# A decoder layer's context maxima reduced over the partitions by TensorE and two small transfers, and the second half's x transposed through another PSUM bank

## The chip, the core and the metric

The kernel runs on one core of a Trainium2 chip. The number that counts is the device time of one execution in microseconds (us). Five engines share the work: PE (TensorE, matrix products and transpositions), DVE (VectorE), ACT (ScalarE), POOL (GpSimd) and SP, which here only issues transfers. Each runs its own program in order; they meet at semaphores. PSUM has eight banks, `bank[0]` to `bank[7]`, into which PE writes and which DVE and ACT read.

## What is computed

One pre-norm decoder layer over x of 4 batches by 512 tokens by 512 channels, in float32:

```python
x = x + attention(layernorm(x), wq, wk, wv, wo)   # 32 query heads, 8 key heads, causal, rotary
x = x + cross(layernorm(x), ctx)                  # below
x = x + moe(layernorm(x), ...)                    # 8 experts and a shared one

def cross(x, w):                                  # w is ctx: 4 matrices of 512x512
    amax = max(abs(xb), axis=-1)                  # per row, blocks of 128
    xq = round_to_fp8(xb * 448 / amax) * amax / 448
    amax = max(abs(wb), axis=(2, 4))              # one maximum for each 128x128 block of ctx
    wq = round_to_fp8(wb * 448 / amax) * amax / 448
    return einsum("emk,enk->emn", xq, wq)
```

The change touches the maxima of the 128x128 blocks of ctx, and the layer norm's transposition of x for the attention of batches 2 and 3.

## The kernel before, in words

**Steps.** The attention is a loop over `h` from -8 to 134, written out in every engine's program; one pass is called a step here, and step `h` works on several heads at once. There are 128 pairs of a head and a batch (below: heads), in 32 units of four heads (`NU`). In step h, PE computes the scores of head h in four pieces (L435, L436), six of the products for the coming unit's queries, keys and values over a unit's four steps of three (L417 to L419 from `XT`, `Wh`, `Wl`), the weighted values of head h-3 (`weigh`, L474, L475, into bank 5), the transpositions of the probabilities of head h-2 (`turn_p`, L459, parts 0, 1 and 2 in banks 2, 3 and 4) and the output product of head h-7 (`attn_out`, L417 to L419 from `Oh`, into bank 5). DVE begins step h with the reciprocal of head h-1's sums (L1027), which makes the start of that row the mark of a step in what follows; then it masks the scores (L1038), joins the weighted values (`join`, L1073), splits the turned probabilities (L1079), rotates queries (L1051) and adds the output product to X (L1088). ACT takes exponentials (L762) and the high parts of splits. POOL scales the probabilities (`normalised`, L1444, four instructions for a head), and takes the low parts of several splits. Nothing plans this order: it is what the loops say, and the semaphores (`need.wait_ge`) hold it together. A counter such as `v_x` is raised by one for each output product added to X.

**The maxima of ctx.** 16 tiles of ctx are loaded into `xnx` one after another. `context_max` (L1112, DVE) takes the maximum of each row in four blocks, into `wam`, 128 partitions by 64. After the last, POOL in step 45 makes the maximum over all partitions of all 64 columns with one `partition_all_reduce` (L1577), so that every partition has all 64 maxima in `wsc`. In step 49 DVE makes scales and their inverses of them (`context_scales`, L1091 to L1096). They are first needed in step 62 (`scaled`, L784).

**x of batches 2 and 3.** `XT[0]` holds the transposed x of batches 0 and then 2, `XT[1]` of 1 and then 3. In steps 51 to 58 DVE normalises one tile of 128 tokens (`first_norm`, L987, into `xnx`), in steps 52 to 59 PE transposes it (`first_turn`, L414, recorded on L409, four transpositions), and ACT (L713) and DVE (L1009) split it into `XT`. The transposition goes into bank 5, just after `attn_out` wrote into the same bank: so it waits until DVE has added that product to X (`wait_bank5`, user "first_turn", L367). In the next step `weigh` writes bank 5 and waits for the split (L374). Unit 16, whose products begin in step 56, needs the four tiles of batch 2 (`wait_xt` in `project`, L485), and unit 17, in step 60, those of batch 3.

**SP.** In each unit it issues the transfers that put keys and queries in place: `turn_keys`, `place_queries` twice (eight issues each), `double_keys`, besides loads of weights.

Of the kernel before, what the change touches and what calls it, by code (L numbers as in the profile page):

```python
# [15 lines left out]
NCTX = 16  # L16
NSAVE = NG


# [59 lines left out]
def decoder(nc, x_in, ctx_in, wqkv_in, wo_in, wg_in, wf_in, ident_in, mask_in, rope_in, ksin_in, rank_in, tri_in, out):  # L79
# [3 lines left out]
    with ExitStack() as root:  # L83
        scope = [root]

        def sem(name):
            return root.enter_context(nc.semaphore(name))

        def sb(name, shape, dt=F32):
# [91 lines left out]
        kept = nc.dram_tensor("kept", (NCTX * 128, D), F32).ap()  # L181
        saved = nc.dram_tensor("saved", (NSAVE, 2, 128, 4, 384), F32).ap()
        oe = nc.dram_tensor("oe", (NE * CAP, D), F32).ap()
        G = [XN[:, k, :] for k in range(TB)] + CW + T1
# [28 lines left out]
            sem(f"v_{n}") for n in ("own", "xn", "xt", "wq", "wo", "ri", "mask", "ra", "rb", "k1", "vl", "join", "pt", "x"))  # L213
        v_bm, v_bq, g_badd, g_bq = sem("v_bm"), sem("v_bq"), sem("g_badd"), sem("g_bq")
        v_cmax, v_cscale, v_q, v_turn, v_x2, v_xn3, v_lt, v_cum, v_place, v_idx, v_piece, v_hm, v_h, v_x3, v_out = (
            sem(f"v_{n}") for n in ("cmax", "cscale", "q", "turn", "x2", "xn3", "lt", "cum", "place", "idx", "piece",
                                    "hm", "h", "x3", "out"))

        g_own, g_pad, g_wq, g_wo, g_norm, g_rot, g_ql, g_ks, g_k, g_kl, g_o, g_zero, g_call, g_t2, g_q, g_const, g_piece = (
            sem(f"g_{n}") for n in ("own", "pad", "wq", "wo", "norm", "rot", "ql", "ks", "k", "kl", "o", "zero", "call", "t2", "q",  # L220
                                    "const", "piece"))
# [139 lines left out]
        def wait_bank5(need, h, user):  # L361

            if user == "attn_out":
                need.wait_ge(a_tmp, h - 2)
                need.wait_ge(v_join, h - 2)
            elif user == "first_turn":
                need.wait_ge(v_x, h - 6)  # L367
            elif h == 3:
                wait_xt(need, 6)
            elif h < 8 or h - 8 >= NH - 11:  # L370
                need.wait_ge(a_tmp, h - 3)
                need.wait_ge(v_join, h - 3)
            elif 52 <= h - 1 < 60:
                wait_xt(need, h - 44)  # L374
            else:
                need.wait_ge(v_x, h - 7)
# [26 lines left out]
        def tensor_engine(e):  # L403
# [34 lines left out]
            def turn_v(u):  # L438
# [8 lines left out]
                last.then_inc(p_vt, 1)  # L447

            def turn_p(h, part):
                ps = bank[2 + part]  # L450
                need.wait_ge(g_norm, 4 * h + 4)
                if h:
                    need.wait_ge(a_pt, 3 * (h - 1) + part + 1)
                    need.wait_ge(v_pt, 3 * (h - 1) + part + 1)
                else:
                    wait_xt(need, 2 * TB)
                for m, (kb, qb) in enumerate(PT_BLOCKS[part]):
                    src = P[:, h % 3, off[qb] + kb * 128:off[qb] + (kb + 1) * 128]
                    last = e.transpose(ps[:, tokens(m)], src, ident[:, :])  # L459
                last.then_inc(p_pt, 1)  # L460
# [189 lines left out]
            for h in range(-8, NH + 7):  # L650
# [22 lines left out]
                if after_unit and k == 1:  # L673
                    need.wait_ge(v_vl, unit)
                if 0 <= h - 2 < NH:
                    turn_p(h - 2, 2)
# [9 lines left out]
                if 52 <= h < 60:  # L686
                    wait_bank5(need, h, "first_turn")
                    first_turn(h - 44, 5)
            for s in (-8, -7, -6):
# [15 lines left out]
        def scalar_engine(e):  # L705
# [172 lines left out]
            for h in range(-8, NH + 7):  # L878
# [48 lines left out]
                if 52 <= h < 60:  # L927
                    first_turn(h - 44, 5)
                if h > NH + 2:
# [26 lines left out]
        def vector_engine(e):  # L956
# [153 lines left out]
            def context_max(m):  # L1110
                need.wait_ge(d_by[m % 2], 16 * (m // 2 + 1))
                e.tensor_reduce(wam[:, m, :], four(xnx[:, m % 2, :]), AX.X, ALU.max,  # L1112
                                apply_absolute_value=True).then_inc(v_cmax, 1)

            def context_scales():
                need.wait_ge(g_call, 1)
                scales(wsc[:, 0, :], wsc[:, 1, :], wsc[:, 0, :], 1e-6).then_inc(v_cscale, 1)
# [217 lines left out]
            for h in range(-8, NH + 7):  # L1335
# [8 lines left out]
                if h in takes:  # L1344
                    context_max(takes[h])
                if h == 49:
                    context_scales()
# [27 lines left out]
                if 0 <= h - 2 < NH:  # L1375
                    pt_lo(h - 2, 1)
                    pt_lo(h - 2, 2)
                if unit < NU and k in (1, 2):
                    rotate(unit, k - 1, 0)
# [12 lines left out]
                if 52 <= h < 60:  # L1392
                    first_turn(h - 44, 5)
                if h > NH + 2:
# [25 lines left out]
        def gpsimd_engine(e):  # L1420
# [129 lines left out]
            for h in range(-8, NH + 7):  # L1550
# [22 lines left out]
                if unit < NU and k == 3:  # L1573
                    rotate(unit)
                if h == 45:
                    need.wait_ge(v_cmax, NCTX)
                    e.partition_all_reduce(wsc[:, 0, :], wam[:, :, :].rearrange("p i c -> p (i c)"), 128,  # L1577
                                           bass.bass_isa.ReduceOp.max).then_inc(g_call, 1)
                if h - 4 in begins:
# [31 lines left out]
        def sync_engine(e):  # L1611
# [138 lines left out]
            for h in range(-8, NH + 7):  # L1750
# [28 lines left out]
                if h in begins:  # L1779
                    load_background(NCTX + begins[h])  # L1780
                if 8 <= h < 24:
                    need.wait_ge(g_zero, 1)
                    e.dma_start(xdz[h - 8], Zb[:, 0, :]).then_inc(d_zero, 16)
# [106 lines left out]
```

## Time and profile before

| what | us |
|---|---|
| median of 3 runs | 1612.51 |
| lowest, highest | 1610.12, 1615.79 |
| the profiled execution | 1612.85 |
| its span in the trace | 1611.0 |
| of it the attention's steps, first to last reciprocal | from 62.5 to about 1040 |

The rest of the time, 1.85 us in the profiled execution, lies around the span. The attention's steps take about 60% of the span; behind them come the cross product and the experts, where the change alters nothing. In the trace a row of an engine tells when an instruction started, how long it took, and in brackets how long the engine had been idle before it and what it waited for.

### The profile page before, as it was taken

What the parts mean: (1) busy time and instruction counts of PE and PEld (TensorE: products, weight loads), DVE (VectorE), ACT (ScalarE), POOL (GpSimd) and SP (SyncE); (2) the same over time, 40 slices, a digit from 0 to 9 for tenths busy, and PEclk for the clock granted to TensorE, in tenths of its full rate; (3) what the DMA queues carried; (4) which work ended last, traced back from release to release, by engine and by line L of the source; (5) the groups of instructions that cost most, each with busy time, mean ns of one, the idle gap of its engine ahead of it and who ended that gap; (6) DMA issues with size and microseconds to landing.
All of it is one profiled execution on the core that took longest, in us unless ns stands there. A gap on an engine that the chain in (4) does not pass through costs nothing.

```text
span 1611.0 us, 26917 instructions
## 1 busy us (share of the span) xinstructions
PE 1465.1 (91%) x8616; PEld 1280.9 (80%) x8616; DVE 1213.7 (75%) x2951; ACT 948.4 (59%) x2384; POOL 1020.4 (63%) x1007
## 2 busy tenths in 40 slices
PE   5799999999798999999999998676989899899997
PEld 4588888887677888888888887565788888799996
DVE  6678888887777777878878787986767665587785
ACT  2477787776466678877878878523121213565662
POOL 1687887885776788888888888642303132354555
PEclk9899999999899999999999999897899999899998
DMA  5345444333132334334434433123010002577777
GB/s 188 98 126 165 135 134 134 109 87 100 49 102 50 88 85 118 98 90 115 113 81 109 120 81 89 33 88 91 27 27 27 8 27 84 176 240 221 227 217 239
DMA packets 106588, 177.04 MB, mean 110 GB/s; under 512 B 16662, under 2 KB 38422, under 8 KB 106448
## 3 DMA queue, kind: packets, MB, share of 16 engines
q1 hardware_dynamic: 103888, 167.07, 35.8%
q0 software_dynamic: 2560, 8.25, 1.6%
q8 instruction: 70, 1.15, 0.3%
q14 instruction: 70, 0.57, 0.1%
HBM read 97.28 MB, written 31.98 MB: 80 GB/s over the span
## 4 chain that ended last, share of the span: by engine, by line
PE 68%; DVE 14%; ACT 7%; issue 5%; DMA 2%; POOL 2%; SPq 1%; DVEq 0%; ACTq 0%; POOLq 0%
PE bank L417 15%; PE bank L419 14%; PE bank L418 14%; PE bank L459 6%; PE bank L435 4%; PE bank L474 4%; PE bank L475 4%; PE bank L436 4%; ACT P L762 3%; PE bank L409 2%; DVE P L1038 2%; DVE Opair L1073 1%; ACT xnx L784 1%; DVE work L987 1%; ACT Otmp L768 1%
## 5 line engine op out<-in xcount | busy, mean ns | idle before, releaser
L762 ACT ACTIVATE P<-P,mn 128x512 f32<-128x512 f32 (+3 forms) x512 | 285.0, 557 | 222.5 <-DVE mn L1038 218.9
L1444 POOL TENSOR_TENSOR P<-P,ri 128x128 f32<-128x128 f32 (+3 forms) x512 | 360.2, 735 | 30.2 <-DVE ri L1027 30.2
L1038 DVE CUSTOM_DVE_ANT_0 P<-bank,mask 128x512 f32<-128x512 f32 (+3 forms) x512 | 236.7, 481 | 117.6 <-PE bank L436 116.0
L1079 DVE TENSOR_TENSOR PTl<-bank,PTh 128x512 fp32r<-128x512 f32 (+1 forms) x384 | 229.6, 599 | 33.4 <-ACT PTh L774 30.8
L459 PE MATMUL bank<-ident,P 128*128 128x128 f32 x1280 | 204.7, 275 | 6.9 <-POOL P L1444 6.9
L435 PE MATMUL bank<-KT,QT 128*128 128x256 f32 (+2 forms) x512 | 190.7, 373 | 17.5 <-DVE mn L1038 17.3
L774 ACT ACTIVATE PTh<-bank 128x512 fp32r<-128x512 f32 (+1 forms) x384 | 197.4, 515 | 12.9 <-PE bank L459 10.0
L417 PE MATMUL bank<-XT,Wh 128*128 128x512 f32 x384 | 166.0, 432 | 11.1 <-DVE qcs L1051 6.2
L474 PE MATMUL bank<-PTh,VS 128*128 128x256 f32 (+2 forms) x512 | 163.6, 330 | 13.0 <-DVE PTl L1079 8.7
L436 PE MATMUL bank<-KT,QT 128*128 128x256 f32 (+2 forms) x512 | 167.7, 328 | 0.0
L459 PEld LDWEIGHTS bank<-ident,P 128*128 128x128 f32 x1280 | 151.8, 141 | 7.7 <-POOL P L1444 7.6
L475 PE MATMUL bank<-PTl,VS 128*128 128x256 f32 (+2 forms) x512 | 156.6, 328 | 0.0
L418 PE MATMUL bank<-XT,Wh 128*128 128x512 f32 x384 | 154.9, 403 | 0.0
L419 PE MATMUL bank<-XT,Wl 128*128 128x512 f32 x384 | 154.4, 402 | 0.0
L1482 POOL TENSOR_TENSOR OTl<-Opair,OTh 128x512 fp32r<-128x512 f32 x64 | 83.4, 1303 | 109.9 <-ACT OTh L802 109.1
L1524 POOL TENSOR_TENSOR Ul<-RW,Uh 128x512 fp32r<-128x512 f32 x50 | 71.3, 1429 | 109.3 <-ACT Uh L829 109.3
L435 PEld LDWEIGHTS bank<-KT,QT 128*128 128x128 f32 x512 | 98.1, 192 | 34.5 <-DVE mn L1038 21.5
L474 PEld LDWEIGHTS bank<-PTh,VS 128*128 128x128 f32 x512 | 97.8, 191 | 28.3 <-ACT PTh L774 9.2
L1487 POOL TENSOR_TENSOR work<-work 128x512 f32<-128x512 f32 x16 | 20.8, 1299 | 153.3 <-DVE work L1108 153.3
L417 PE MATMUL bank<-Oh,OTh 128*128 128x512 f32 x256 | 105.2, 411 | 13.2 <-DVE Opair L1073 5.6
L851 ACT ACTIVATE hm<-bank 128x256 f32<-128x256 f32 x96 | 36.4, 379 | 131.3 <-PE bank L419 131.0
L417 PE MATMUL bank<-XT,Uh 128*128 128x256 f32 x352 | 101.3, 288 | 8.0 <-issue 6.5
(194 smaller groups left out, 4237.8 us busy)
## 6 DMA issues: line engine op xcount, KB each, us to landing
RW<-in_wf SPq DMA_DIRECT2D x170, 256.0 KB, 3.1
QT<-qh SPq DMA_DIRECT2D x256, 64.0 KB, 2.0
QT<-ql SPq DMA_DIRECT2D x256, 64.0 KB, 2.0
Oraw<-in_wo SPq DMA_DIRECT2D x16, 512.0 KB, 5.3
KT<-KT SPq DMA_DIRECT2D x32, 256.0 KB, 3.0
xnx<-in_ctx SPq DMA_DIRECT2D x32, 256.0 KB, 3.4
Wraw<-in_wqkv SPq DMA_DIRECT2D x9, 768.0 KB, 5.3
saved<-Wh SPq DMA_DIRECT2D x7, 768.0 KB, 3.5
```

What stands on the lines that cost most here:

```text
L417: e.matmul(ps, lh, rh, start=start, stop=False)
L418: e.matmul(ps, lh, rl, start=False, stop=False)
L419: return e.matmul(ps, ll, rh, start=False, stop=stop)
L435: e.matmul(ps[:, 0:k], lhs, KT[:, u % 2, 0, 0:k], start=True, stop=False)
L436: e.matmul(ps[:, 0:k], lhs, KT[:, u % 2, 1, 0:k], start=False, stop=True).then_inc(p_s, 1)
L459: last = e.transpose(ps[:, tokens(m)], src, ident[:, :])
L474: e.matmul(ps[:, q:512], lhs, pt_of(PTh, kb), start=kb == 0, stop=False)
L475: last = e.matmul(ps[:, q:512], lhs, pt_of(PTl, kb), start=False, stop=kb == 3)
L762: e.activation(pq, pq, ACT.Exp, bias=mn[:, z, qb:qb + 1], scale=-1.0, accum_out=rs[:, z, qb:qb + 1]).then_inc(a_exp, 1)
L1038: e.tensor_tensor_reduce(P[:, z, off[qb]:off[qb] + k], bank[n % 2][:, 0:k], mask[:, 512 - k:512], -0.125, BIG, ALU.add, ALU.min, mn[:, z, ...
L1079: e.tensor_tensor(pt_part(PTl, part), bank[2 + part][:, 0:128 * n].rearrange("p (m n) -> p m n", n=128), pt_part(PTh, part).bitcast(F32), ...
L1444: e.tensor_tensor(pq, pq, ri[:, z, qb:qb + 1].to_broadcast([128, n]), ALU.mult).then_inc(g_norm, 1)
```

## The change

First, the maxima over the partitions. POOL's `partition_all_reduce` goes. In step 46 (`AT_PEAK`) PE transposes `wam` (128 by 64) into the free half of bank 4 (64 partitions by 128), DVE takes one maximum for each of the 64 partitions into a column of `wsc` (`context_peak`), SP writes these 64 numbers to DRAM in step 48 and reads them back in step 49, all 64 into each of the 128 partitions. `context_scales` moves from step 49 to step 51.

Second, x of batches 2 and 3 is transposed into bank 2, the bank of part 0 of the turned probabilities, instead of bank 5. The transposition in step h waits for the split of part 0 of head h-2, and part 0 of the next head waits for the split of x. `weigh` and `attn_out` have bank 5 to themselves.

```diff
--- before.py
+++ after.py
@@ -15,6 +15,7 @@
 CHUNK_BANK = (4, 5, 7)
 NCTX = 16
 NSAVE = NG
+AT_PEAK = 46
 
 
 class Once:
@@ -180,6 +181,7 @@
+        peak = nc.dram_tensor("peak", (4 * NCTX,), F32).ap()
@@ -363,15 +366,11 @@
             if user == "attn_out":
                 need.wait_ge(a_tmp, h - 2)
                 need.wait_ge(v_join, h - 2)
-            elif user == "first_turn":
-                need.wait_ge(v_x, h - 6)
             elif h == 3:
                 wait_xt(need, 6)
             elif h < 8 or h - 8 >= NH - 11:
                 need.wait_ge(a_tmp, h - 3)
                 need.wait_ge(v_join, h - 3)
-            elif 52 <= h - 1 < 60:
-                wait_xt(need, h - 44)
             else:
                 need.wait_ge(v_x, h - 7)
 
@@ -446,9 +445,20 @@
                     last = e.transpose(bank[4][:, 256 + 64 * i:320 + 64 * i], kvs[64:128, tokens(i)], ident[64:128, 64:128])
                 last.then_inc(p_vt, 1)
 
+            def turn_maxima():
+
+                need.wait_ge(v_cmax, NCTX)
+                need.wait_ge(a_pt, 3 * (AT_PEAK - 2))
+                need.wait_ge(v_pt, 3 * (AT_PEAK - 2))
+                e.transpose(bank[4][0:64, 256:384], wam[:, :, :].rearrange("p i c -> p (i c)"), ident[:, :]).then_inc(p_cmax, 1)
+
             def turn_p(h, part):
                 ps = bank[2 + part]
                 need.wait_ge(g_norm, 4 * h + 4)
+                if part == 0 and 51 <= h < 59:
+                    wait_xt(need, h - 42)
+                if part == 2 and h == AT_PEAK - 1:
+                    need.wait_ge(v_peak, 1)
                 if h:
                     need.wait_ge(a_pt, 3 * (h - 1) + part + 1)
                     need.wait_ge(v_pt, 3 * (h - 1) + part + 1)
@@ -672,6 +682,8 @@
                     scores(h, 0)
                 if after_unit and k == 1:
                     need.wait_ge(v_vl, unit)
+                if h == AT_PEAK:
+                    turn_maxima()
                 if 0 <= h - 2 < NH:
                     turn_p(h - 2, 2)
                 if unit < NU:
@@ -684,8 +696,9 @@
                         wait_xt(need, t - 5)
                     first_turn(t, (4, 5, 0, 1)[t - TB])
                 if 52 <= h < 60:
-                    wait_bank5(need, h, "first_turn")
-                    first_turn(h - 44, 5)
+                    need.wait_ge(a_pt, 3 * (h - 2) + 1)
+                    need.wait_ge(v_pt, 3 * (h - 2) + 1)
+                    first_turn(h - 44, 2)
             for s in (-8, -7, -6):
                 side_slot(s)
             for x in range(NX - 1):
@@ -925,7 +938,7 @@
                     first_turn(t, (4, 5, 0, 1)[t - TB])
-                    first_turn(h - 44, 5)
+                    first_turn(h - 44, 2)
@@ -1112,8 +1125,13 @@
                 e.tensor_reduce(wam[:, m, :], four(xnx[:, m % 2, :]), AX.X, ALU.max,
                                 apply_absolute_value=True).then_inc(v_cmax, 1)
 
+            def context_peak():
+
+                need.wait_ge(p_cmax, 1)
+                e.tensor_reduce(wsc[0:64, 1, 0:1], bank[4][0:64, 256:384], AX.X, ALU.max).then_inc(v_peak, 1)
+
             def context_scales():
-                need.wait_ge(g_call, 1)
+                need.wait_ge(d_peak[1], 16)
                 scales(wsc[:, 0, :], wsc[:, 1, :], wsc[:, 0, :], 1e-6).then_inc(v_cscale, 1)
 
             def steps_of(j):
@@ -1343,7 +1361,7 @@
                     split_wq_lo(h // 8 + 1)
                 if h in takes:
                     context_max(takes[h])
-                if h == 49:
+                if h == AT_PEAK + 5:
                     context_scales()
                 if h - 2 in begins:
                     steps_of(begins[h - 2])
@@ -1375,6 +1393,8 @@
                 if 0 <= h - 2 < NH:
                     pt_lo(h - 2, 1)
                     pt_lo(h - 2, 2)
+                if h == AT_PEAK:
+                    context_peak()
                 if unit < NU and k in (1, 2):
                     rotate(unit, k - 1, 0)
                 if 0 <= h - 7 < NH:
@@ -1390,7 +1410,7 @@
-                    first_turn(h - 44, 5)
+                    first_turn(h - 44, 2)
@@ -1572,10 +1592,6 @@
                     pair(h - 3)
                 if unit < NU and k == 3:
                     rotate(unit)
-                if h == 45:
-                    need.wait_ge(v_cmax, NCTX)
-                    e.partition_all_reduce(wsc[:, 0, :], wam[:, :, :].rearrange("p i c -> p (i c)"), 128,
-                                           bass.bass_isa.ReduceOp.max).then_inc(g_call, 1)
                 if h - 4 in begins:
                     background_add(begins[h - 4])
                 if h - 5 in begins:
@@ -1778,6 +1794,12 @@
                     keep(begins[h - 7])
                 if h in begins:
                     load_background(NCTX + begins[h])
+                if h == AT_PEAK + 2:
+                    need.wait_ge(v_peak, 1)
+                    e.dma_start(peak.unsqueeze(1), wsc[0:64, 1, 0:1]).then_inc(d_peak[0], 16)
+                if h == AT_PEAK + 3:
+                    need.wait_ge(d_peak[0], 16)
+                    e.dma_start(wsc[:, 0, :], peak.partition_broadcast(128)).then_inc(d_peak[1], 16)
                 if 8 <= h < 24:
                     need.wait_ge(g_zero, 1)
                     e.dma_start(xdz[h - 8], Zb[:, 0, :]).then_inc(d_zero, 16)
```

Four places show how the instructions stand. On PE the end of step 53 and the first half of step 54, before and then after. In it `Oh,OTl` is the end of step 53's output product and `xnx` the normalised tile of x.

```order
L419 MATMUL bank<-Oh,OTl 128x512
L409 MATMUL bank<-ident,xnx 128x128 [waits v_xn,v_x]
L409 MATMUL bank<-ident,xnx 128x128 x3
L435 MATMUL bank<-KT,QT 128x512 [waits v_mask]
...
L419 MATMUL bank<-XT,Wl 128x512
L474 MATMUL bank<-PTh,VS 128x512 [waits a_xt,v_xt,v_pt,a_pt]
L475 MATMUL bank<-PTl,VS 128x512
...
L459 MATMUL bank<-ident,P 128x128 [waits g_norm]
L459 MATMUL bank<-ident,P 128x128 x3
```

```order
L418 MATMUL bank<-Oh,OTl 128x512
L408 MATMUL bank<-ident,xnx 128x128 [waits v_xn,v_pt,a_pt]
L408 MATMUL bank<-ident,xnx 128x128 x3
L434 MATMUL bank<-KT,QT 128x512 [waits v_mask]
...
L418 MATMUL bank<-XT,Wl 128x512
L484 MATMUL bank<-PTh,VS 128x512 [waits v_x,v_pt,a_pt]
L485 MATMUL bank<-PTl,VS 128x512
...
L469 MATMUL bank<-ident,P 128x128 [waits v_xt,a_xt,g_norm]
L469 MATMUL bank<-ident,P 128x128 x3
```

The instructions stand in the same order; the first transposition waits for `v_pt` and `a_pt` (the split of turned probabilities) where it waited for `v_x`, `weigh` (the rows of PTh,VS) waits for `v_x` where it waited for the split of x, and the first row of `turn_p` has that wait now.

On POOL from step 45 to step 46: before, with the reduction (the rows named ISA), then after.

```order
L1444 TENSOR_TENSOR P<-P,ri 128x384
L1444 TENSOR_TENSOR P<-P,ri 128x512
L1577 ISA
L1577 ISA wsc<-wam 128x64 [waits v_cmax]
L1430 ISA
L1430 TENSOR_TENSOR Wl<-Wraw,Wh 128x4x128 [waits p_q,a_wq]
L1444 TENSOR_TENSOR P<-P,ri 128x128 [waits v_ri]
L1444 TENSOR_TENSOR P<-P,ri 128x256
```

```order
L1464 TENSOR_TENSOR P<-P,ri 128x384
L1464 TENSOR_TENSOR P<-P,ri 128x512
L1450 TENSOR_TENSOR Wl<-Wraw,Wh 128x4x128 [waits p_q,a_wq]
L1464 TENSOR_TENSOR P<-P,ri 128x128 [waits v_ri]
L1464 TENSOR_TENSOR P<-P,ri 128x256
```

Three rows are gone: the reduction, and one in front of it and one behind it on the line of the following instruction.

On SP from step 48 to step 50, of after:

```order
L1640 DMA Oraw<-in_wo 128x1024 [waits a_wo,v_wo,g_wo]
L1799 DMA peak<-wsc 64x1 [waits v_peak]
L1678 DMA QT<-qh 32x512 [waits p_s,a_qh]
L1678 DMA QT<-qh 32x512 x7
L1802 DMA wsc<-peak 128x64 [waits d_peak_out]
L1678 DMA QT<-ql 32x512 [waits g_ql]
L1678 DMA QT<-ql 32x512 x7
L1686 DMA KT<-KT 64x1024 [waits g_kl,a_kh]
```

The two rows with `peak` are new. The read stands between the eight transfers of the queries' high part and the eight of the low part.

On DVE, the start of step 51 of after; before, the rows with `wsc` stood behind the reciprocal of step 49, and the first of them waited for `g_call`:

```order
L1101 TENSOR_TENSOR X<-X,bank 128x512 [waits v_x,p_ao]
L1040 RECIPROCAL ri<-rs 128x4 [waits a_exp]
L1104 TENSOR_SCALAR wsc<-wsc 128x64 [waits d_peak_in]
L1106 RECIPROCAL wsc<-wsc 128x64 [waits v_own]
L1108 TENSOR_SCALAR wsc<-wsc 128x64 [waits v_own]
L1109 TENSOR_SCALAR wsc<-wsc 128x64
L1051 ISA P,mn<-bank,mask 128x512 [waits p_pt,p_s]
L1051 ISA mn 128x1
```

## Rows read from the trace of the kernel before

**Rows 1.** The page: busy time of each engine over the span

```profile
PE 1465.1 (91%) x8616; PEld 1280.9 (80%) x8616; DVE 1213.7 (75%) x2951; ACT 948.4 (59%) x2384; POOL 1020.4 (63%) x1007
```

**Rows 2.** Windows: start:end, us, busy (instructions) by engine; PEclk, DMA share, GB/s

```profile
323.40:375.19 51.79, 51.79 (x296) 45.09 (x296) 42.82 (x114) 38.40 (x100) 43.01 (x45) 1.00 0.33 85
382.17:452.47 70.30, 57.15 (x299) 48.96 (x299) 51.56 (x117) 38.38 (x100) 43.08 (x46) 0.93 0.23 59
588.81:655.22 66.41, 66.12 (x380) 57.21 (x379) 53.78 (x146) 53.11 (x142) 57.41 (x60) 1.00 0.37 98
452.47:536.45 83.98, 71.98 (x408) 60.12 (x407) 60.89 (x157) 54.64 (x135) 54.41 (x57) 0.98 0.22 61
```

**Rows 3.** Timeline of POOL, 380 to 404: start, us, instruction, idle before

```profile
394.57 0.54 POOL L1577 PARTITION_ALL_REDUCE wsc<-wam  x1 [5.80 <-issue]
401.82 1.25 POOL L1430 TENSOR_TENSOR Wl<-Wraw,Wh 128x512 fp32r<-128x512 f32 x1 [6.71 <-issue]
```

**Rows 4.** Timeline of PE, 404 to 434, its rows with idle time

```profile
405.84 1.11 PE L459 MATMUL bank<-ident,P 128*128 128x128 f32 x4 [6.46 <-POOL P L1444]
...
419.82 0.38 PE L435 MATMUL bank<-KT,QT 128*128 128x256 f32 x1 [3.91 <-DVE mn L1038]
...
431.39 0.39 PE L435 MATMUL bank<-KT,QT 128*128 128x256 f32 x1 [2.02 <-DVE mn L1038]
```

**Rows 5.** Timeline of DVE, 412 to 431

```profile
412.70 6.46 DVE L1017 TENSOR_TENSOR Wl<-Wraw,Wh 128x512 fp32r<-128x512 f32 x1
...
426.16 1.01 DVE L1091 TENSOR_SCALAR wsc<-wsc 128x64 f32<-128x64 f32 x1
...
428.34 2.39 DVE L1096 TENSOR_SCALAR wsc<-wsc 128x64 f32<-128x64 f32 x1
```

**Rows 6.** A window of 2 us, the granted clock third from the end

```profile
490.00:492.00 2.00, 2.00 (x6) 1.57 (x5) 1.15 (x5) 1.41 (x4) 2.00 (x3) 0.50 0.60 163
```

**Rows 7.** Waits in 452.47 to 536.45: who for whom, us, times, longest

```profile
PE bank L409 <- DVE X L1088: 10.5, 8, 1.6
```

**Rows 8.** Timeline of PE around step 55, and the start of step 60

```profile
485.02 0.39 PE L419 MATMUL bank<-Oh,OTl 128*128 128x512 f32 x1
486.80 0.66 PE L409 MATMUL bank<-ident,xnx 128*128 128x128 f32 x4 [1.38 <-DVE X L1088]
487.21 0.48 PE L435 MATMUL bank<-KT,QT 128*128 128x512 f32 x1
...
489.06 0.63 PE L417 MATMUL bank<-XT,Wh 128*128 128x512 f32 x1 [0.80 <-DVE XT L1009]
...
528.63 0.47 PE L417 MATMUL bank<-XT,Wh 128*128 128x512 f32 x1 [0.65 <-issue]
```

**Rows 9.** Timeline of DVE at the same two places

```profile
486.06 0.68 DVE L1088 TENSOR_TENSOR X<-X,bank 128x512 f32<-128x512 f32 x1
486.66 0.96 DVE L987 TENSOR_SCALAR xnx<-X,mv,rstd 128x512 f32<-128x512 f32 x1
488.12 0.69 DVE L1009 TENSOR_TENSOR XT<-bank,XT 128x512 fp32r<-128x512 f32 x1 [0.50 <-ACT XT L713]
...
525.78 0.68 DVE L1088 TENSOR_TENSOR X<-X,bank 128x512 f32<-128x512 f32 x1
```

**Rows 10.** Timeline of DVE at the start of step 43

```profile
367.85 0.17 DVE L1027 RECIPROCAL ri<-rs 128x4 f32<-128x4 f32 x1
...
368.51 0.68 DVE L1038 CUSTOM_DVE_ANT_0 P<-bank,mask 128x512 f32<-128x512 f32 x1
```

**Rows 11.** PE: step 43's first score piece, and the first that needs the mask

```profile
366.20 0.39 PE L435 MATMUL bank<-KT,QT 128*128 128x512 f32 x1
...
370.06 0.36 PE L435 MATMUL bank<-KT,QT 128*128 128x256 f32 x1
```

**Rows 12.** POOL in that step

```profile
368.42 2.77 POOL L1444 TENSOR_TENSOR P<-P,ri 128x128 f32<-128x128 f32 x4
```

**Rows 13.** The page, transfers: size and us from issue to landing

```profile
QT<-qh SPq DMA_DIRECT2D x256, 64.0 KB, 2.0
```

More of the change, by code:

```diff
@@ L214, in decoder @@
         v_bm, v_bq, g_badd, g_bq = sem("v_bm"), sem("v_bq"), sem("g_badd"), sem("g_bq")
+        p_cmax, v_peak, d_peak = sem("p_cmax"), sem("v_peak"), [sem("d_peak_out"), sem("d_peak_in")]
         v_cmax, v_cscale, v_q, v_turn, v_x2, v_xn3, v_lt, v_cum, v_place, v_idx, v_piece, v_hm, v_h, v_x3, v_out = (
@@ L217, in decoder @@
                                     "hm", "h", "x3", "out"))
-        g_own, g_pad, g_wq, g_wo, g_norm, g_rot, g_ql, g_ks, g_k, g_kl, g_o, g_zero, g_call, g_t2, g_q, g_const, g_piece = (
-            sem(f"g_{n}") for n in ("own", "pad", "wq", "wo", "norm", "rot", "ql", "ks", "k", "kl", "o", "zero", "call", "t2", "q",
+        g_own, g_pad, g_wq, g_wo, g_norm, g_rot, g_ql, g_ks, g_k, g_kl, g_o, g_zero, g_t2, g_q, g_const, g_piece = (
+            sem(f"g_{n}") for n in ("own", "pad", "wq", "wo", "norm", "rot", "ql", "ks", "k", "kl", "o", "zero", "t2", "q",
                                     "const", "piece"))
```

## The prediction, made before the changed kernel ran

> **What bounds the kernel now.** I read the page first: PE is busy for 91% of the span, no other engine for more than 75% [rows 1]. That share is a mean, so I looked for stretches in which PE isn't the bound, with the reciprocals of DVE (L1027) as marks of the steps. In undisturbed attention PE is never idle: steps 37 to 43 take 51.79 us with 51.79 busy, at full clock, and steps 68 to 76 take 66.41 with 66.12 busy [rows 2]. The same steps of their cycle of eight, where the change lies, are longer: steps 45 to 51 take 70.30 us, 18.5 more than 51.79, and steps 52 to 60 take 83.98, 17.6 more than 66.41 [rows 2]. So 36 us are all that can be had here, and of it PE's own eight sets of transpositions stay. Next I read who waited, in these two stretches alone.
>
> **First stretch, the reduction.** POOL ends head 44's probabilities 5.80 us before it starts the reduction at 394.57; its next instruction comes at 401.82, 6.71 us of idle time behind it [rows 3]. The rows give no releaser ("issue"). 5.80 + 0.54 + 6.71 = 13.0 us in which POOL scales no probabilities. PE stands before `turn_p` for 6.46 us of it [rows 4]; the rest was room that POOL had. The lateness is paid twice more. In step 48 DVE's split of Wl takes 6.46 us, while POOL works through its backlog, and PE waits 3.91 us for masked scores; in step 49 the scales take from 426.16 to 430.73, 4.57 us, and PE waits 2.02 [rows 4, 5]. After the two long gaps the clock is at its lower level, 1.2 instead of 2.4 GHz (0.50 granted) in windows like that of [rows 6]. The mean of 0.93 over the 70.30 us [rows 2] leaves out 7% of PE's speed, 4.9 us, of which I take 4 for lost, since PE idles in part of it. 6.5 + 3.9 + 2.0 + 4 = 16.4, and some small waits make up the 18.5.
>
> All of this starts with the reduction, and the change takes it away with the two rows that stand beside it in POOL's order. What it adds:
> - PE: one transposition with `wam`. Four for x start 0.41 us before the next product [rows 8], so 0.1 us, on the path. Its waits are those that part 2 of `turn_p` behind it has anyway.
> - DVE: one maximum of 64 by 128 in step 46. A mask over 128x512 takes 0.68 [rows 10] and this is a quarter of its width; I take 0.3 us, hidden, since DVE has time left in undisturbed steps (42.82 busy in 51.79) [rows 2]. Without this cover it would cost 0.3.
> - SP: two issues, in steps 48 and 49. The trace has no transfer of 4 bytes per partition. The nearest row are the 64 KB of queries, 2.0 us to landing [rows 13]; from above I let it be 10 us, from below nothing. A wait for the first on SP holds the eight transfers of the queries' low part and the doubled keys, which the scores of step 52 need. But the write is issued a step (7.4 us) before the read, and the read over one step before DVE wants it; even 10 us each would hold SP for 3, and the queries have two steps. I take no cost.
> - DVE: the scales stand in step 51 now. How much DVE may be late there, the start of step 43 shows (the same place of the cycle): masking begins 0.66 us after the reciprocal's start, the score piece that needs it starts 2.21 after it [rows 10, 11]. Masking takes 0.6, so 0.95 is left, and with the maximum in front of the mask gone (0.57) about 1.5. POOL is at its four probabilities from 0.57 to 3.34 us of the step [rows 10, 12], and the scales took 4.57 us in such company [rows 5]. From below: a 128x64 operation that isn't held takes some 0.2 to 0.5 us (0.55 for the reciprocal's row between those shown), in all 1.1, all hidden. From above: DVE gets nothing until 3.3, then 0.4 more, 3.8 of delay, 2.3 us for PE. I take 3.3 of delay, near the upper end because [rows 5] is a direct look: 1.8 us for PE.
>
> The Trainium skill (SBUF — State Buffer, "SBUF: two separate sides") says that DVE instructions of some kinds and POOL instructions exclude each other on a shared pair of ports, the loser waiting for the winner's whole instruction. 2.39 us of [rows 5] agrees, since it ends with a POOL instruction; the 6.46 us does not quite: several POOL instructions went by. By the page alone the scales would be late by less, and PE would wait some 1 us in place of 1.8.
>
> Sum of this stretch: 18.5 - 0.1 - 1.8 = **16.6 us** less.
>
> **Second stretch, x through bank 2.** PE waits 10.5 us in eight places for the output product to be added to X before it transposes x [rows 7]; one is the 1.38 of step 55 [rows 8]. In after it waits for the split of part 0 of the turned probabilities, which DVE does before the last scores' mask, so before this add; that wait is over when PE arrives. The transpositions stay (8 x 0.41 = 3.3 us).
> - Six of the eight gaps aren't in front of a new unit. The two that are have 1.38 each, so six have 10.5 - 2.8 = 7.7 us. What is late next is DVE: it must add, normalise, split and mask the next scores. From the start of the add, 0.60 + about 0.9 + 0.6 + 0.1 + 0.6 = 2.8 us [rows 9, 10], and the add starts 0.8 us behind the output product's end (486.06 against 485.25 by the next start on PE) [rows 8, 9]. PE wants that mask 0.4 (x) + 3.9 us [rows 11] after the same end, 4.3 against 3.6. So 0.7 us is in hand, and I take the whole **7.7**. In DVE's sum: 60.89 busy in nine steps is 6.8 a step, with waits of some 0.5 to 0.8 that no order removes, against PE's 7.4 + 0.4. It is close.
> - Step 55 to 56. Unit 16 needs the split of this very step. Before, PE idled 1.38 and then 0.80 [rows 8]. In after the transposition is early, but DVE's chain is not: add from 486.06, normalise to about 487.6, split 0.6 to 488.2, and PE could go on at 488.5 in place of 489.06. **0.5** gained, and one gap of 1.6 in place of two.
> - Step 59 to 60, unit 17: no tile is normalised in step 59, so the split follows the add: 525.78 + 0.6 + 0.6 + 0.1 = 527.1 in place of 528.6 [rows 8, 9]. **1.4** gained.
> - The clock is low at 490 [rows 6], behind the two gaps of step 55/56; a product of 512 columns takes 0.63 us there against 0.39 [rows 8]. The mean of 0.98 over 83.98 us [rows 2] makes 1.7 us, and I take 1.6. A single gap of 2.02 at 431.39 [rows 4] was followed by products at full clock. One of 1.6 is shorter, so I count **1.6** as gained; the bound on the other side is nothing.
> - `weigh` waits for `v_x` of the step before, as in every undisturbed step. Part 0 of `turn_p` in steps 53 to 60 waits for the split of x, done 1.3 us or more before PE gets there, by the same sum. Nothing.
>
> Sum: 7.7 + 0.5 + 1.4 + 1.6 = **11.2 us** less, 83.98 down to 72.8.
>
> **Forecast.** The profiled execution took 1612.85 us, span and what lies around it; the median is 1612.51, so the two stand for each other. 1612.85 - 16.6 - 11.2 = 1585 us. Nothing behind step 60 changes, and PE is the bound there until the attention ends, so no other stage gives it back.
>
> **Rivals.**
> - *DVE takes over in the second stretch.* Each tile is normalised in 0.58 to 0.96 us, the longer one next to POOL's work [rows 9]. If DVE, with fewer pauses, is held for one POOL instruction of 1.3 us in each of seven steps, it loses 9 us, of which some 5 are in hand; the clock falls at step 56 as before (1.6), and the scales cost the 2.3 of the upper bound. 1585 + 4 + 1.6 + 0.5 = **1591**. For it speaks the row of 6.46 us; against it that DVE then stood against a backlog.
> - *Everything clean.* The scales hide, no wait is left at step 56: 1585 - 1.8 - 1.6 = **1581.5**.
> - *The transfers land late.* DVE then stands at its first scale in step 51, ten us behind the read's issue. With 27 us to the landing of the read, 15 us of PE's time are gone beyond what is in hand: **1600**.
> - *Slower than before.* The same place, longer: SP waits for the write of 64 pieces of 4 bytes, behind it on SP stand the queries of unit 13, and every score of step 52 waits for those. From the write in step 48 to the scores of step 52 are four steps, 29 us, of which the transfers behind it need some 9 (eight issues, 2.0 and a few us more for the keys); so 20 us are free, and beyond that each us costs one. From 20 + 28 = 48 us to landing the kernel is slower than before; with 55 us it would take **1620**. Transfers of 2.0 us on the same queue [rows 13] speak against it.
> - *The change does not do what it says*, the stall of POOL sits on something else than the reduction. POOL's order of after has none of the three rows, so I see no place for it; only the second part would then be had: **1602**.
>
> The Trainium skill (GPSIMD Engine Reference, "Instruction dispatch") gives the load of code for the first call of such a function as about 6 us. The 5.80 us agrees; it says nothing on the 6.71 us behind. By the page alone POOL's stall would be 6 us, and with it about half of the first stretch's gain, 1593 in all; the row has both gaps, and I go by the row.
>
> **How the numbers follow.** Forecast 0.62; DVE takes over 0.15; clean 0.10; late transfers 0.05; slower 0.03; change without its effect 0.05. A difference of 0.3% (4.8 us) is about what a measurement of this kernel can tell from none. Faster by more: all but the slower case and some of what I haven't thought of, 0.95; within 0.02; slower 0.03. The range takes in the forecast, the clean case and DVE taking over, with the 2 or 3 us by which runs differ: 1580 to 1593.
>
> **What would show it.** Right: POOL has no gap over 6 us near 390; DVE's split of Wl in step 48 takes a fraction of 6.46 us; steps 45 to 51 take 53 to 54 us; PE waits at most once for DVE there, in step 51. Steps 52 to 60 take 72 to 74 us, with PE waiting only in front of units 16 and 17. Wrong: idle time of PE in front of `turn_p` part 0 or of the first score piece in steps 53 to 59 (DVE is the bound), or a wait of DVE for the transfer in step 51.

## The result, and the profile after

| | before | after |
|---|---|---|
| median, us | 1612.3 (4 runs, 1610.1 to 1615.8) | 1586.74 (4 runs, 1585.0 to 1590.7) |
| profiled execution, its span | 1612.85, 1611.0 | 1584.99, 1583.2 |
| steps 45 to 51 | 70.30 | 54.49 |
| steps 52 to 60 | 83.98 | 73.76 |
| steps 62 to 127 | 500.05 | 500.03 |

The ratio is 0.9843, 95% interval 0.9816 to 0.9869: 25.6 us faster, where 27.8 were forecast (1585 us, range 1580 to 1593). A stretch of steps is again taken from one DVE reciprocal (now L1040) to another. The two stretches give 15.8 + 10.2 = 26.0 of the 27.8 us between the two spans. 1.1 us of the rest was already gone when step 45 opened (381.06 for 382.17), where both kernels do the same; between executions such differences come and go.

The windows of the two stretches in after, to be read against [rows 2] (start:end, us, busy by engine, PEclk, DMA share, GB/s):

```profile
381.06:435.55 54.49, 53.14 (x301) 46.06 (x301) 44.63 (x119) 38.26 (x100) 43.73 (x45) 1.00 0.30 77
435.55:509.31 73.76, 69.60 (x407) 59.21 (x406) 61.05 (x157) 53.73 (x135) 54.64 (x57) 1.00 0.25 70
```

PE is at full clock in both. It is idle for 1.35 us of the first (13.2 before) and 4.16 us of the second (12.0). POOL's timeline where [rows 3] had two gaps of 5.80 and 6.71 us has none:

```profile
384.91 2.75 POOL L1464 TENSOR_TENSOR P<-P,ri 128x128 f32<-128x128 f32 x4
387.97 1.30 POOL L1450 TENSOR_TENSOR Wl<-Wraw,Wh 128x512 fp32r<-128x512 f32 x1 [0.31 <-ACT Wh L737]
389.22 2.77 POOL L1464 TENSOR_TENSOR P<-P,ri 128x128 f32<-128x128 f32 x4
```

DVE's timeline: the split of Wl in step 48, 6.46 us in [rows 5], and the four operations on the scales, 4.57 us there:

```profile
403.38 1.19 DVE L1030 TENSOR_TENSOR Wl<-Wraw,Wh 128x512 fp32r<-128x512 f32 x1
...
425.65 0.17 DVE L1040 RECIPROCAL ri<-rs 128x4 f32<-128x4 f32 x1
425.73 0.57 DVE L1104 TENSOR_SCALAR wsc<-wsc 128x64 f32<-128x64 f32 x1
426.34 0.55 DVE L1106 RECIPROCAL wsc<-wsc 128x64 f32<-128x64 f32 x1
426.93 0.31 DVE L1108 TENSOR_SCALAR wsc<-wsc 128x64 f32<-128x64 f32 x1
427.16 0.87 DVE L1109 TENSOR_SCALAR wsc<-wsc 128x64 f32<-128x64 f32 x1
427.94 0.68 DVE L1051 CUSTOM_DVE_ANT_0 P<-bank,mask 128x512 f32<-128x512 f32 x1
```

All rows of PE with idle time from step 45 to the start of step 61, in place of [rows 4, 7, 8]:

```profile
428.69 0.39 PE L434 MATMUL bank<-KT,QT 128*128 128x256 f32 x1 [0.58 <-DVE mn L1051]
431.56 0.47 PE L416 MATMUL bank<-Oh,OTh 128*128 128x512 f32 x1 [0.77 <-DVE Opair L1086]
455.37 0.47 PE L416 MATMUL bank<-Oh,OTh 128*128 128x512 f32 x1 [0.45 <-DVE Opair L1086]
463.58 0.47 PE L416 MATMUL bank<-Oh,OTh 128*128 128x512 f32 x1 [0.38 <-DVE Opair L1086]
468.46 0.47 PE L416 MATMUL bank<-XT,Wh 128*128 128x512 f32 x1 [2.01 <-DVE XT L1022]
497.67 0.47 PE L416 MATMUL bank<-Oh,OTh 128*128 128x512 f32 x1 [0.37 <-DVE Opair L1086]
501.51 0.47 PE L416 MATMUL bank<-XT,Wh 128*128 128x512 f32 x1 [0.95 <-issue]
```

The waits for X are gone. What is left in steps 52 to 60 stands in front of units 16 and 17 (2.01 and 0.95), as forecast, and three times in front of output products (Opair, the joined values), which was not forecast. In step 51 PE waits twice for DVE, where one wait was forecast. The two transfers, in the view of transfers (size, us to landing):

```profile
wsc<-peak SPq DMA_DIRECT2D x1, 32.0 KB, 3.4
peak<-wsc SPq DMA_DIRECT2D x1, 0.2 KB, 7.3
```

The write was issued at 405.98 and the read at 415.64, behind the eight transfers of queries; so the write had landed 2.4 us before the read's turn, and the read 6.7 us before DVE's first scale. Neither was waited for.

### The profile page after: what moved, and what is told of

It is laid out like the page before. It is cut to its first block, busy times and chain, and to the rows that moved or that the text cites. A ratio compares the mean times of both kernels' runs of the same rounds, so it can differ in the third digit from the quotient of the medians.

```text
span 1583.2 us, 26919 instructions
## 1 busy us (share of the span) xinstructions
PE 1452.8 (92%) x8617; PEld 1270.5 (80%) x8617; DVE 1207.7 (76%) x2952; ACT 948.1 (60%) x2384; POOL 1021.4 (65%) x1006
## 4 chain that ended last, share of the span: by engine, by line
PE 69%; DVE 15%; ACT 8%; issue 4%; DMA 2%; POOL 2%; SPq 0%; DVEq 0%; ACTq 0%; POOLq 0%
PE bank L416 15%; PE bank L417 14%; PE bank L418 14%; PE bank L469 6%; PE bank L434 4%; PE bank L484 4%; PE bank L485 4%; PE bank L435 4%; ACT P L775 3%; DVE P L1051 2%; PE bank L408 2%; ACT xnx L797 1%; DVE Opair L1086 1%; ACT Otmp L781 1%; DVE work L1000 1%
```

## Experiments

The times of steps come from one profile of each. The experiments ran on three chips, on which "before" had medians of 1611.35 (e1 to e4), 1610.82 (e5 to e8) and 1611.95 us (e9 to e12). "PE idle" is the length of steps 52 to 60 less PE's busy time in them, gaps too short for a row of their own included; PEclk is of these steps too.

| run | median | 45-51 | 52-60 | PE idle | PEclk | 45-61 |
|---|---|---|---|---|---|---|
| before | 1612.3 | 70.30 | 83.98 | 12.00 | 0.98 | 162.16 |
| after | 1586.7 | 54.49 | 73.76 | 4.16 | 1.00 | 136.12 |
| e1, maxima alone | 1597.2 | 54.44 | 82.51 | 12.19 | 1.00 | 144.82 |
| e2, bank 2 alone | 1601.7 | 70.33 | 75.39 | 4.12 | 0.98 | 153.60 |
| e3, reduction twice | 1611.7 | 71.67 | 82.47 | 12.03 | 1.00 | 162.02 |
| e4, old wait kept | 1597.6 | 54.45 | 85.41 | 13.82 | 0.98 | 147.74 |
| e5, scales in step 61 | 1585.7 | 52.40 | 73.84 | 4.12 | 1.00 | 134.94 |
| e6, split first | 1585.5 | 54.46 | 74.18 | 4.11 | 1.00 | 136.51 |
| e7, copy first | 1587.2 | 54.46 | 74.95 | 4.16 | 0.98 | 137.28 |
| e8, all three | 1586.2 | 52.40 | 75.25 | 3.89 | 0.98 | 136.34 |
| e9, small norm | 1587.2 | 54.46 | 72.65 | 3.15 | 1.00 | 134.98 |
| e10, scales inside 61 | 1586.3 | 52.41 | 75.38 | 4.14 | 0.98 | 136.06 |
| e11, norm on ACT | 1590.1 | 53.40 | 75.56 | 3.17 | 0.98 | 136.83 |
| e12, both last | 1589.8 | 51.32 | 74.19 | 3.17 | 1.00 | 134.05 |

**The two parts apart.** e1 is the changed kernel with x turned in bank 5 again, e2 the kernel before with x turned in bank 2; the edits are the change's own hunks.

> Only the first part of the change: maxima by transposition and transfers, x still turned in bank 5. If the two parts are independent, steps 45 to 51 take 54.5 us as in the changed kernel (70.3 before) and steps 52 to 60 keep about 84 us: about 1612.3 - 16 = 1596 us. Rival: part of the first stretch's gain is only had because the second part takes over DVE's lateness of step 51; then this run gives 1600 or more.

> Only the second part: POOL's reduction stays, x turned in bank 2. Independent parts: steps 45 to 51 keep 70 us, steps 52 to 60 take 74 us in place of 84, about 1602 us. Rival: the lateness behind the reduction reaches step 52 and DVE has no room there, then steps 52 to 60 take 76 us or more.

Measured: e1 0.9909 (0.9886 to 0.9933), 14.1 us less; e2 0.9945 (0.9927 to 0.9964), 9.7 us less. Together 23.8, and the whole change 25.6. Each stretch of steps gets its own part's gain, whatever the other does: 54.44 and 54.49, 70.33 and 70.30. The parts are independent, and both rivals fall: e2's 75.39 has the lower clock in it (0.98), and its waits are those of after (0.39, 0.39, 2.01, 0.36, 0.97). What e1 does not separate is the reduction from the move of the scales from step 49, where PE waited 2.02 us behind them, to step 51.

**What POOL waits for at the reduction.** e3 is the kernel before with these lines behind the reduction, and the scales wait for both:

```diff
+                    need.wait_ge(g_call, 1)
+                    e.partition_all_reduce(wsc[:, 0, :], wam[:, :, :].rearrange("p i c -> p (i c)"), 128,
+                                           bass.bass_isa.ReduceOp.max).then_inc(g_call, 1)
```

> The kernel before with the same reduction made twice, the second right behind the first (same result). If the two gaps of POOL (5.80 us ahead, 6.71 us behind) are paid for changing to another set of functions and back, the second reduction adds only its own time, 1 to 2 us of POOL, and the kernel takes 1613 to 1616 us. Rival: the time behind the reduction is its own work that the row of 0.54 us doesn't show; then POOL is held for another 6.7 us or more, PE waits that much longer, and it takes 1619 us or more.

POOL's timeline of e3:

```profile
394.09 0.54 POOL L1577 PARTITION_ALL_REDUCE wsc<-wam  x1 [5.66 <-issue]
394.73 0.52 POOL L1580 PARTITION_ALL_REDUCE wsc<-wam  x1
402.81 1.25 POOL L1430 TENSOR_TENSOR Wl<-Wraw,Wh 128x512 fp32r<-128x512 f32 x1 [7.55 <-issue]
```

The second reduction starts 0.64 us behind the first, and the gap behind both is 7.55 in place of 6.71 us. One reduction costs POOL about 1.5 us (0.64 + 0.84), and its stretch of steps 1.4 us. The forecast of 1613 to 1616 us for the whole was missed: the ratio is 1.0004 (0.9994 to 1.0015), from 1 us less to 2.4 us more, so 1.4 us can't be told from nothing there. The rival's 1619 us is excluded. So some 11.5 of the 13 us are paid once, ahead of the first reduction and behind the last. That they are paid for a change to what the reduction needs and back fits this, but no row shows what is done in that time.

**The wait for the add, alone.** e4 is the changed kernel with one line more in front of the transposition of x into bank 2:

```diff
                     need.wait_ge(v_pt, 3 * (h - 2) + 1)
+                    need.wait_ge(v_x, h - 6)
                     first_turn(h - 44, 2)
```

> The changed kernel, but the transposition of x into bank 2 also waits, as before the change, for the output product to be added to X. If that wait is what the second part takes away, it brings back 10 us of idle time of PE on the transposition's line and steps 52 to 60 take about 83 us: 1596 us. Rival: DVE is the bound of these steps anyhow, then most of that idle time only moves and steps 52 to 60 take 76 to 78 us.

PE's waits from step 52 to 60 in e4:

```profile
PE bank L408 <- DVE X L1102: 12.4, 8, 1.8
PE bank L416 <- DVE XT L1023: 0.8, 1, 0.8
PE bank L416 <- issue: 0.7, 1, 0.7
```

The wait brings back all of it and more: 85.41 us, 1.6 of them by the clock, so some 1.3 us over e1's 82.51 at full clock. The new bank by itself gives nothing; it is the way to be rid of the wait. Where the 1.3 us come from stays open.

**What is left in step 51.** e5 moves the scales to the start of step 61, e10 behind the second mask of step 61, where DVE is idle. The edit of e5:

```diff
-                if h == AT_PEAK + 5:
+                if h == 61:
                     context_scales()
```

> The changed kernel with DVE's four operations on the scales moved from step 51 to step 61, one step before their first use. If these 2.3 us of DVE cost PE its two waits of step 51 (0.58 us for the mask, 0.77 us for the joined values) and nothing in step 61, where the mask has 2.4 us of room, steps 45 to 61 take 1.3 us less than in the changed kernel (136.1 us). Rival: DVE's lateness is the same wherever it falls, steps 45 to 61 take the same 136 us within 0.3.

> The changed kernel with the scales in step 61, behind the second mask, where DVE is idle for 2.0 us, in place of the start of step 51. At the start of step 61 they moved 0.8 us into that step. Theory: in the pause they cost PE 0.3 us or less, steps 45 to 61 take 134.2 us (136.1 in the changed kernel, 134.9 with them at the start of step 61). Rival: POOL's long instructions at that place hold them beyond the pause, and 135 us or more.

e5: both waits of step 51 vanish (52.40 us, all of it PE busy), and steps 45 to 61 take 1.2 us less, as expected. Step 61 gets 0.8 longer by its marks, but PE is idle for only 0.10 of it, and step 62 gets 0.4 shorter (6.90 for 7.31): most of it is the mark at the end, which DVE sets late. PE's idle time from step 45 to 61 falls by 1.3 us, from 5.51 to 4.22. e10: the same 52.41, and step 61 takes 8.27 us where it took 7.87 in after and 8.70 in e5, with 0.03 us of PE's idle time. Its sum of 136.06 misses the expected 134.2 by the clock: step 56 takes 11.00 us where it takes 9.45 in e5. Without that 1.6 it would be 134.5; that is my reckoning, not a measurement.

**What is left in steps 52 to 60.** e6 lets DVE split the turned x before it normalises the next tile, e7 lets ACT copy the weighted values before the second exponential, e8 has e5, e6 and e7 together. The edits of e6 and e7:

```diff
-                if 51 <= h < 59:
-                    first_norm(h - 43)
                 if 52 <= h < 60:
                     first_turn(h - 44, 2)
+                if 51 <= h < 59:
+                    first_norm(h - 43)
```

```diff
                     exp(h, 3)
-                    exp(h, 2)
+                    if not 53 <= h < 60:
+                        exp(h, 2)
                 if 0 <= h - 3 < NH:
                     lower_out(h - 3)
+                if 53 <= h < 60:
+                    exp(h, 2)
```

> The changed kernel with DVE's split of the turned x ahead of the normalisation of the next tile, in steps 52 to 59. In step 55 the split then ends some 0.9 us earlier, and PE's wait of 2.01 us in front of unit 16 falls to about 1.1 us; that of 0.95 us in front of unit 17 stays, since step 59 has no normalisation. Steps 52 to 60 take 72.9 us in place of 73.8. Rival: ACT's half of the split is late, so DVE stands and waits for it, and nothing or less than 0.3 us is gained.

> The changed kernel, but ACT in steps 53 to 59 copies the lower half of the weighted values before the second exponential in place of after it. If the three waits of 0.45, 0.38 and 0.37 us in front of the output product come by mask, two exponentials, copy and join, they vanish and steps 52 to 60 take 1.2 us less (72.6 us). Rival: the copy waits for PE's weighted values at that place and delays the exponential; then the waits stay or grow.

> The changed kernel with all three: scales in step 61, split before normalisation, copy before the second exponential. If the three costs are separate, steps 45 to 61 take 136.1 - 1.3 - 0.9 - 1.2 = 132.7 us and the kernel some 3.4 us less than the changed one. Rival: DVE's total work is the bound in steps 53 to 59 and takes back what each alone gives; then 134 us or more.

None of e6 to e8 gave what I expected. In e6 the wait in front of unit 16 does fall, to 1.19 us, but the one for the joined values in step 55 grows to 0.78:

```profile
457.90 1.53 DVE L1000 TENSOR_SCALAR xnx<-X,mv,rstd 128x512 f32<-128x512 f32 x1
...
462.20 0.68 DVE L1086 TENSOR_TENSOR Opair<-bank,Otmp 64x512 f32<-64x512 f32 x1 [0.68 <-ACT Otmp L781]
```

The normalisation now stands where POOL works, and takes 1.53 us for 0.86, so the next masks are late by that. In e7 the waits for the joined values vanish, and the waits in front of the units grow from 2.01 and 0.95 to 2.47 and 1.55: PE's idle time is 4.16 us in all, as in after. e8 has 136.34 us where 132.7 were expected and its rival said 134 or more; without the 1.5 us of the clock in step 56 it has e5's gain alone. What PE waits for moves, its sum hardly does (4.16, 4.11, 4.16, 3.89). That points at the chain of DVE and ACT as what sets the pace of these steps, and not the place where PE happens to stand; the next three runs ask how much of it is DVE's work.

**Is it DVE's work?** e9 shortens the normalisation (first diff; it leaves out 480 of the 512 columns of the normalised x in six tiles, so its result is not the layer's), e11 gives it to ACT (second diff, in ACT's program; `nmr` is the negative mean times `rstd`, made by DVE before step 0), e12 is e11 with the scales as in e10:

```diff
+                if t > 2 * TB + 1:
+                    e.tensor_scalar(xn[m][:, 0:32], X[:, t, 0:32], mv[:, t, 0:1], rstd[:, t:t + 1], ALU.subtract,
+                                    ALU.mult).then_inc(v_xn, 1)
+                    return
                 normed(xn[m], t).then_inc(v_xn, 1)
```

```diff
+            def first_norm(t):
+                need.wait_ge(v_nmr, 1)
+                need.wait_ge(p_xt, t - 1)
+                need.wait_ge(v_cmax, NCTX)
+                e.activation(xn[xn_of(t)], X[:, t, :], ACT.Identity, bias=nmr[:, t:t + 1],
+                             scale=rstd[:, t:t + 1]).then_inc(a_xn, 1)
```

> The changed kernel with DVE's normalisation of x cut to 32 of 512 columns for the tiles of steps 53 to 58 (it leaves out most of the normalised x of these tiles). Theory: in steps 53 to 59 DVE's own work sets the pace, with PE's idle time only the place where it shows; 0.5 to 0.8 us less DVE work in six steps makes steps 52 to 60 3 to 4 us shorter (70 to 71 us in place of 73.8), and PE's waits in front of the output product go. Rival: PE's path over the split of x sets it; then only the wait in front of unit 16 gets shorter and it takes 72.8 us or more.

> The changed kernel with the normalisation of x of batches 2 and 3 on ACT (scale and bias), which has time left, in place of DVE. If DVE's work sets the pace of steps 53 to 59, steps 52 to 60 take 70 to 71 us in place of 73.8, and the wait in front of unit 16 falls from 2.0 to about 1.1 us: about 1583.5 us. Rival: ACT's 0.7 us delay its part of the split as much as DVE gains, and it takes 73 us.

> The two last together: normalisation on ACT and the scales inside step 61. If they add up, steps 45 to 61 take 136.1 - 3 - 1.9 = 131 us and the kernel takes about 1582 us. Rival: ACT or PE is now the bound, and one of the two gives nothing (133 us or more).

e9: 72.65 us, 1.1 less, PE idle for 3.15 in place of 4.16; of the waits for joined values 0.18 us is left, and of those in front of the units 1.76 and 0.95. That is the rival's figure (72.8 or more) rather than mine (70 to 71), though the rival left the waits for joined values standing. My 3 to 4 us would have needed nearly all of PE's 4.16 us of idle time, with the waits in front of the units, and those hang on PE's own transposition and the split behind it. e11: the waits for joined values are gone, the one in front of unit 16 is 1.90, since ACT's part of the split is late now, as its rival said; 75.56 us has the lower clock, and the mark in front of it stands earlier, because DVE no longer normalises in step 51. PE's idle time is 3.17 us in both e11 and e12, as in e9. So whether DVE's work is cut or moved, PE gets back 1.0 of its 4.16 us; what stays stands in front of the units. Steps 45 to 61 take 136.83 us in e11 with the lower clock, and 134.05 in e12 without it, 2.1 less than after, where 131 were expected and the rival said 133 or more. But the profiled execution of e12 is its fastest, 1584.38 us for a median of 1589.8. In time neither is better: the ratios to before are 0.9858 (0.984 to 0.9876) and 0.9862 (0.9845 to 0.9879), against 0.9843 of the change and 0.9836 to 0.9847 of e5 to e10. No version here beats the changed kernel by what can be measured.

## Why the prediction was right, and where by luck

- *POOL's stall goes, and what hangs on it.* Right. The split of Wl takes 1.19 us, the low clock behind it is gone, steps 45 to 51 take 54.49 us where 53.7 follow from the sum, just over the 53 to 54 named as a sign. The 4 us for the clock were right: PE is busy for 4.0 us less (53.14 for 57.15). e3 supports the reading that the stall is paid for the visit, not for the work.
- *The scales in step 51.* A term sized wrongly twice. I took 3.3 us of delay on DVE, 1.8 for PE. DVE needed 2.30 us. My 3.3 took [rows 5] for a look at the same company, POOL's four probabilities; it was another. POOL beside the scales of before, and beside those of after (two of the four probabilities by themselves):

```profile
425.82 1.30 POOL L1482 TENSOR_TENSOR OTl<-Opair,OTh 128x512 fp32r<-128x512 f32 x1 [3.63 <-ACT OTh L802]
427.08 1.29 POOL L1430 TENSOR_TENSOR Wl<-Wraw,Wh 128x512 fp32r<-128x512 f32 x1
428.32 2.35 POOL L1456 TENSOR_TENSOR ql<-qcs,qh 128x1024 fp32r<-128x1024 f32 x1
...
424.96 1.29 POOL L1502 TENSOR_TENSOR OTl<-Opair,OTh 128x512 fp32r<-128x512 f32 x1 [2.16 <-ACT OTh L815]
426.57 0.61 POOL L1464 TENSOR_TENSOR P<-P,ri 128x256 f32<-128x256 f32 x1
427.14 0.83 POOL L1464 TENSOR_TENSOR P<-P,ri 128x384 f32<-128x384 f32 x1
```

  Each TENSOR_SCALAR of the scales ends 0.05 us behind one of these: at 427.17, 428.42 and 430.73 before, at 426.30, 427.24 and 428.03 in after. Each is held for the one POOL instruction beside it, and the probabilities are short. By the sum, with 2.30 in place of 3.3, PE should have lost 0.8. It lost 0.58 in front of the mask's piece, and 0.77 in front of the output product: the late mask delays ACT's two exponentials, which stand ahead of the copy of the weighted values, which DVE's join needs. The step of the prediction that failed is "what is late next": it followed DVE to the next scores and left out ACT. e5 shows that both waits come from the scales. Some more of the 2.7 us over 51.79 is only the later mark at the end.
- *Six gaps go whole, 7.7 us.* Nearly: 6.5 of the 7.7 us. The three waits of 0.45, 0.38 and 0.37 us (steps 54, 55 and 59) are of the same kind, by mask, exponentials, copy and join. The prediction had 0.7 us in hand at the mask, where indeed no wait came, and called it close; the chain through ACT is what it left out here too. Steps 53 to 55 took about 8.2 us each, not 7.8. The first rival, DVE taking over, thus was half true: not by one held instruction in each step, but by a chain through two engines.
- *Units 16 and 17.* Forecast waits of 1.6 and 0.6 us, measured 2.01 and 0.95; together 0.8 more. The rows of steps 55 and 59 were taken over with DVE's start of the add, 0.8 us behind the end of the output product; in after it starts 1.0 us behind it (466.05 and 500.13, against 465.05 and 499.14). That is half of the difference. The rest is mostly PE being there sooner: with no wait in front of it the transposition starts 0.16 us ahead of the product's modelled end (465.05 for 465.21).
- *The clock, 1.6 us.* Right in after, but not shown to be the change's doing. In before the clock fell behind gaps of 1.38 and 0.80 us in steps 55 and 56 [rows 6, 8]. e1 has the same two gaps (1.39 and 0.80) and keeps it, by the windows of these steps:

```profile
471.00:473.00 2.00, 1.20 (x6) 0.81 (x5) 1.62 (x4) 0.83 (x2) 0.77 (x2) 1.00 0.02 4
473.00:475.00 2.00, 2.00 (x13) 1.73 (x12) 1.41 (x5) 1.42 (x4) 2.00 (x3) 1.00 0.66 141
```

  With one wait of 2.01 us it stayed in after and fell in e2 and e10. In these profiles it costs 1.5 us or so where it falls, and no rule on the gap's length tells when: it fell in 7 of the 14 profiles. At the same clock the second part gives 82.5 - 73.8 = 8.7 us. What I should have written is 9.6 for the second part and the 1.6 as half a chance.
- *The transfers.* No cost, right. But the write took 7.3 us to land (7.3 to 7.7 in the eleven kernels that have it), more than three times the nearest row. The 10 us I had allowed covered it; with the read one step earlier SP would have stood.
- Sum: 16.6 + 11.2 forecast, 15.8 + 10.2 measured in the steps, 14.1 and 9.7 by the medians of the parts alone. The two signs "at most one wait for DVE, in step 51" and "only in front of units 16 and 17" did not come true. That 1585 lies 1.7 us from the median is closer than the terms deserve.

## What to carry to other kernels

A short special function on POOL can cost over twenty times its own row: read the idle time on both sides of it, then follow the queue that stood behind it, since here, of a stall of 13 us, PE stood for only 6.5 itself, and the steps around it became 15.8 us shorter with it gone. A transposition and a small transfer over DRAM replace a maximum over partitions at almost no cost in time, if whoever needs it can wait for some steps: in e5 PE is never idle in steps 45 to 51. When a wait is taken away, follow every engine that stands in the chain to the next wait, not the nearest one alone; and before a second repair, compare its hoped-for gain with the idle time that is left.

## What the runs showed of the hardware that I had not expected

- The idle time behind the reduction (6.71 us) is longer than the one ahead (5.80), and a second reduction in a row costs about 1.5 us.
- Writing 64 pieces of 4 bytes to DRAM took 7.3 to 7.7 us from issue to landing in the eleven kernels that do it; reading 256 bytes into each of 128 partitions took 3.1 to 3.4 us, and 64 KB of queries 2.0.
- The Trainium skill (SBUF — State Buffer, "SBUF: two separate sides") says that the loser of the ports waits for the winner's whole instruction. For the scales the trace agrees, for one instruction of POOL each: in all 14 profiles a TENSOR_SCALAR of theirs that is held ends 0.05 us behind a POOL instruction, from 0.31 us beside the short ones to 2.39 beside the one of 2.35. The 6.46 us of [rows 5] is against the plain reading: that one instruction of DVE stood while seven of POOL went by without a pause,

```profile
412.16 1.27 POOL L1449 TENSOR_TENSOR qcs<-qcs,q2s 128x512 f32<-128x512 f32 x1
413.40 1.28 POOL L1450 TENSOR_TENSOR qcs<-qcs,q2s 128x512 f32<-128x512 f32 x1
414.64 2.74 POOL L1444 TENSOR_TENSOR P<-P,ri 128x128 f32<-128x128 f32 x4
417.36 1.25 POOL L1462 TENSOR_TENSOR krot<-krot,ksin 64x512 f32<-64x512 f32 x1
```

  where in after the same one took 1.19 us and let only one POOL instruction go by. Both ended 0.55 us behind POOL (419.16 for 418.61, 404.57 for 404.02). What decides between the two, no run here tells.
- The clock's fall after the same idle times is not the same from run to run: it fell in before and not in e1, both with idle times of 1.4 and 0.80 us.
